# Attention with a mixture of experts: the order of work between the last query tile and the first routed tile

## What is computed

```python
attn = softmax(q_rounded @ k_rounded.T)          # per head, rows of 2048 keys
attn = round to 0..255 steps of the row's maximum
x = x + (attn @ v_rounded) @ Wp + bp
```

```python
logits = h @ router_w.T
scores = sqrt(softplus(logits)); idx = top_k(scores + expert_bias, 4)
out = sum over chosen e of share[e] * swiglu(h; gate_e, up_e, down_e)   # inner width 256
x = x + out + swiglu(h; shared weights)          # gate and up are clamped to +-7
```

## Time and profile before

| | us |
|---|---|
| median of 3 runs (1398.88 to 1402.76) | 1398.91 |
| profiled execution, reported time | 1404.4 |
| its span | 1402.7 |
| TensorE, VectorE busy | 1208.6 (86%), 1100.1 (78%) |
| ScalarE, GpSimd busy | 941.7 (67%), 884.2 (63%) |
| one gate copy (L902), one hidden product (L908), mean | 0.691, 0.453 |

### The profile page before, as it was taken

The page is one execution under the profiler, slowest core; times in us unless marked ns, Lnnn a source line. Parts: engine busy times, 40 slices in busy tenths (PEclk is TensorE's granted clock), DMA queues, the critical chain, the costliest instruction groups (busy, mean ns, idle before and its releaser), DMA issues.

```text
span 1402.7 us, 29359 instructions
## 1 busy us (share of the span) xinstructions
PE 1208.6 (86%) x7437; PEld 602.6 (43%) x7535; DVE 1100.1 (78%) x2282; ACT 941.7 (67%) x1349; POOL 884.2 (63%) x910
## 2 busy tenths in 40 slices
PE   7999577888888888888888855666999999999995
PEld 3444134444454444545444433333444444444442
DVE  4567899999999999999999964474667676767673
ACT  2224398999999999999999975212555555555552
POOL 3122388998889898989899972413445454545443
PEclk9999899999999999999999977877999999999997
DMA  7565878877777777767776773925678887787442
GB/s 256 127 152 128 165 128 159 151 144 154 141 140 147 153 148 145 147 145 142 146 153 135 158 176 101 305 29 205 134 204 214 248 231 172 183 243 187 86 66 30
DMA packets 401186, 220.10 MB, mean 157 GB/s; under 512 B 357335, under 2 KB 357463, under 8 KB 401122
## 3 DMA queue, kind: packets, MB, share of 16 engines
q1 hardware_dynamic: 380786, 180.51, 53.7%
q0 software_dynamic: 20336, 38.83, 15.5%
HBM read 101.88 MB, written 40.89 MB: 102 GB/s over the span
## 4 chain that ended last, share of the span: by engine, by line
PE 49%; issue 20%; DVE 14%; POOL 7%; ACT 5%; DMA 3%; SPq 1%; DVEq 0%; POOLq 0%; ACTq 0%
PE psS L1408 19%; PE psS L870 11%; DVE mem L623 5%; DVE mem L639 5%; POOL mem L713 4%; PE psS L474 4%; PE psS L1855 3%; ACT mem L580 3%; PE psAV L1842 1%; DMA mem<-mem 1%; PE psP L854 1%; PE psAV L520 1%; POOL mem L696 1%; PE psP L424 1%; PE psS L862 1%
## 5 line engine op out<-in xcount | busy, mean ns | idle before, releaser
L580 ACT ACTIVATE mem<-mem 128x2048 uint8<-128x2048 f32 x256 | 534.0, 2087 | 33.9 <-POOL mem L696 29.4
L713 POOL TENSOR_SCALAR mem<-mem 128x2048 bf16<-128x2048 uint8 x256 | 485.8, 1898 | 31.2 <-DMA mem<-mem 10.7
L474 PE MATMUL psS<-mem 128*128 128x512 bf16 x928 | 290.5, 387 | 88.0 <-DVE mem L639 36.8
L639 DVE TENSOR_SCALAR_CACHE_REDUCE mem<-psS,mem 128x1024 f32<-128x1024 f32 x256 | 327.3, 1279 | 3.5 <-PE psS L474 3.5
L623 DVE TENSOR_SCALAR_CACHE_REDUCE mem<-psS 128x1024 f32<-128x1024 f32 x256 | 312.3, 1220 | 12.8 <-PE psS L474 10.3
L1408 PE MATMUL psS<-mem 128*128 x624 | 296.1, 597 | 0.0
L1296 POOL DMA_INDIRECT out_y<-mem x78 | 123.5, 1584 | 191.9 <-DVE mem L1485 101.3
L870 PE MATMUL psS<-mem 128*128 (+1 forms) x376 | 191.2, 633 | 7.1 <-ACT mem L884 7.1
L494 PEld LDWEIGHTS psAV<-mem 128*128 128x128 bf16 x4096 | 139.4, 96 | 90.0 <-issue 26.6
L474 PEld LDWEIGHTS psS<-mem 128*128 128x128 bf16 x1024 | 72.2, 98 | 217.6 <-DVE mem L623 124.2
L902 DVE TENSOR_SCALAR mem<-psS 128x512 f32<-128x512 f32 x81 | 56.0, 691 | 138.2 <-PE psS L1408 117.1
(11 more groups left out here) (225 smaller groups left out, 1332.6 us busy)
## 6 DMA issues: line engine op xcount, KB each, us to landing
mem<-in_moe_w SPq DMA_DIRECT2D x64, 768.0 KB
xn_dram<-mem SPq DMA_DIRECT2D x29, 256.0 KB, 2.3
mem<-in_x SPq DMA_DIRECT2D x28, 256.0 KB, 3.0
mem<-xn_dram SPq DMA_DIRECT2D x19, 256.0 KB, 3.0
mem<-mem SPq DMA_TRANSPOSE x292, 3.1
mem<-in_ctx_in SPq DMA_DIRECT2D x16, 256.0 KB, 3.7
out_y<-mem SPq DMA_DIRECT2D x16, 256.0 KB, 2.2
gated_dram<-mem SPq DMA_DIRECT2D x13, 256.0 KB, 2.2
```

Source lines behind the costliest of these rows:

```text
L474: last = nc.tensor.matmul(psS[c][:, k * D:(k + 1) * D], qT[pm][:, hm, :], kT[:, hm, c * HALF + k * D:c * HALF + (k + 1) * D], start=True, ...
L580: nc.scalar.activation(p8[slot], S[slot], ACT.Exp, bias=NB[:, slot:slot + 1], scale=sq[p][:, h:h + 1], accum_out=Z[p][:, h:h + 1]).then_in ...
L639: nc.vector.tensor_scalar(S[before][:, HALF:TK], psS[1][:], 1.0, M[:, 2 * before:2 * before + 1], ALU.mult, ALU.max, accum_out=M[:, 2 * be ...
L713: nc.gpsimd.tensor_scalar(pb[slot], pT[slot].bitcast(U8).rearrange("p (j q b) -> p j b q", b=2, q=P), 1.0, 0.0, ALU.mult, ALU.add).then_in ...
```

## The change

On TensorE, the finish of tile 15 comes first in the run-out. The up product of tile 13 is made at l = 0, that of tile 14 at l = 14, that of tile 15 after the last step, all from the router's transposed rows xn2T and the weights gate_w that the attention stage uses; the reloads, `pe_tokens` and the copies for tiles 13 to 15 go. Of the other shared work only the transposes of hidden tile 0 (l = 7) and 1 (l = 28) stay in the run-out; the other hidden transposes and all sixteen down products come after it, with the ranks after k = 2, the ends after k = 5, and the lists 0 and 1 after k = 12 and k = 15. ScalarE takes the first tiles' softplus start ahead of unit 254's exponential. VectorE takes the clamps of tiles 0 to 3, the widening of unit 254, and the router of 13 tiles, then 3. GpSimd skips unit 254, clamps tile k + 6 ahead of add k. SP loads tiles 4 and 5 at l = 5, tiles 6 and 7 at l = 21, and tiles 8 to 12 with the first five experts after the up product of tile 15. Hidden products 6 to 9 take the places of 10 to 12 among the slot steps (7 one step later, 9 after the last sum). The ranks wait for x1 and gate 14, whose banks they use; all renumbered waits in the routed stage are left out here.

```diff
-    EARLY = 6
-    TA = TT - 2
+    TA = TT - 3
+    LAST = TT * H - 1
...
-                pe.wait_ge(probs_ready, n - LAG + 1)
+                if isinstance(n, int) and n - LAG == LAST - 1:
+                    pe.wait_ge(probs_wide, 1)
+                elif isinstance(n, int) and n - LAG == LAST:
+                    pe.wait_ge(probs_ready, LAST)
+                else:
+                    pe.wait_ge(probs_ready, n - LAG + 1)
...
+                if isinstance(t, int) and t >= TT:
+                    act.wait_ge(gu_mm, t - TT + 1)
                 nc.scalar.activation(xn2T.rearrange("p c t -> p (c t)"), psT[:], ACT.Copy).then_inc(router_ev, 1)
...
+            if isinstance(n, int) and n == LAST - 1:
+                act.wait_ge(logits_cp, TA)
+                nc.scalar.activation(absl[:, 0:TA, :], logits[:, 0:TA, :], ACT.Abs).then_inc(r_abs, 1)
+                act.wait_ge(r_abs, 1)
+                nc.scalar.activation(ex[:, 0:TA, :], absl[:, 0:TA, :], ACT.Exp, scale=-1.0).then_inc(r_exp, 1)
...
-            if not isinstance(n, int) or 0 <= n - BEHIND < TT * H:
+            if not isinstance(n, int) or 0 <= n - BEHIND < TT * H and n - BEHIND != LAST - 1:
...
+            if isinstance(k, int) and k < SHARED:
+                if due(k - 1):
+                    pe.wait_ge(hT_ready, k - 1)
+            else:
                 pe.wait_ge(hT_ready, k)
...
+        def bank_up(k):
+            return psT[:] if k == SHARED - 1 else psAV[0][:]
+
+        def pe_up(pe, k):
+            pe.wait_ge(router_ev, k + 1)
+            if k == GATED:
+                pe.wait_ge(x1_ready, TT - 1)
+            elif k == GATED + 1:
+                pe.wait_ge(gu_ready, 1)
             for c in range(DC):
-                last = nc.tensor.matmul(bankG[o], xT[o][:, c, :], w(c * 2 * I, 2 * I), start=(c == 0), stop=(c == DC - 1))
+                last = nc.tensor.matmul(bank_up(k), xn2T[:, c, :], gate_w[c], start=(c == 0), stop=(c == DC - 1))
             last.then_inc(gu_mm, 1)
...
+            if isinstance(k, int) and k < GATED:
+                return xg[k % MU]
+            return gu_third if isinstance(k, int) and k == SHARED - 1 else gu[o]
...
         def pe_early(pe):
             for l in range(PAIR):
                 pe_step(pe, TT // 2, l)
-                if l == 1:
-                    pe.wait_ge(shared_in, 16 * SHARED_PIECES)
+                if l == 0:
+                    pe_up(pe, GATED)
+                if l == LAG:
                     for c in range(2):
                         pe.wait_ge(half_max[c], TT * H)
-                if 2 <= l < 2 + 2 * EARLY:
-                    k = l // 2 - 1
-                    if l % 2 == 0:
-                        pe_hidden(pe, k, k % 2)
-                    else:
-                        pe_down(pe, k, k % 2, shared_weights)
-            pe.wait_ge(router_ev, TT)
-            pe.wait_ge(logits_cp, TT)
-            for k in range(EARLY, GATED):
+                    pe_hidden(pe, 0, 0)
+                if l == 14:
+                    pe_up(pe, GATED + 1)
+                if l == 28:
+                    pe_hidden(pe, 1, 1)
+            pe_up(pe, GATED + 2)
+            pe.wait_ge(shared_in, 16 * SHARED_PIECES)
+            pe_down(pe, 0, 0, shared_weights)
+            for k in range(2, SHARED):
                 pe_hidden(pe, k, k % 2)
-                if k > EARLY:
-                    pe_down(pe, k - 1, (k - 1) % 2, shared_weights)
-                if k == GATED - 4:
+                pe_down(pe, k - 1, (k - 1) % 2, shared_weights)
+                if k == 2:
+                    pe.wait_ge(logits_cp, TT)
+                    pe.wait_ge(x1_ready, TT)
+                    pe.wait_ge(gu_ready, 2)
                     pe_ranks(pe)
-            for k in range(GATED, SHARED):
-                o, before_o = k % 2, (k - 1) % 2
-                pe_tokens(pe, k, k % MU)
-                if k > GATED:
-                    pe_hidden(pe, k - 1, before_o)
-                pe_down(pe, k - 1, before_o, shared_weights)
-                if k == GATED:
-                    pe.wait_ge(hT_ready, GATED)
...
                 if l == 0:
-                    act.wait_ge(logits_cp, TA)
-                    nc.scalar.activation(first(absl), first(logits), ACT.Abs).then_inc(r_abs, 1)
-                    act.wait_ge(r_abs, 1)
-                    nc.scalar.activation(first(ex), first(absl), ACT.Exp, scale=-1.0).then_inc(r_exp, 1)
+                    act.wait_ge(r_plus, 1)
+                    nc.scalar.activation(first(lnu), first(u), ACT.Ln).then_inc(r_ln, 1)
+                if l == 1:
                     for k in range(2):
                         act_silu(act, k, k)
-                if 2 <= l < 2 + 2 * EARLY:
-                    k = l // 2 - 1
-                    if l % 2 == 0:
-                        act_hidden(act, k, k % 2)
-                        if k + 2 < EARLY + 1:
-                            act_silu(act, k + 2, k % 2)
-                    else:
-                        act_early_out(act, k)
-                if l == 3:
-                    act.wait_ge(r_plus, 1)
-                    nc.scalar.activation(first(lnu), first(u), ACT.Ln).then_inc(r_ln, 1)
-                if l == 7:
                     act.wait_ge(r_soft, 1)
                     nc.scalar.activation(first(score), first(full), ACT.Sqrt).then_inc(r_sqrt, 1)
+                if l == 4:
+                    act_hidden(act, 0, 0)
+                if l == 7:
+                    for k in range(2, 4):
+                        act_silu(act, k, k % 2)
+                if l == 27:
+                    act_hidden(act, 1, 1)
...
-            for k in range(EARLY, GATED):
+            act_early_out(act, 0)
+            for k in range(2, SHARED):
+                if k + 2 < SHARED:
+                    act_silu(act, k + 2, k % 2)
                 act_hidden(act, k, k % 2)
-                if k + 1 < GATED:
-                    act_silu(act, k + 1, (k + 1) % 2)
-                if k > EARLY:
-                    act_early_out(act, k - 1)
-            for k in range(GATED, SHARED):
-                act_tokens(act, k, k % 2)
-                if k > GATED:
-                    act_hidden(act, k - 1, (k - 1) % 2)
                 act_early_out(act, k - 1)
-                act_silu(act, k, k % 2)
-            act_hidden(act, SHARED - 1, (SHARED - 1) % 2)
             act_early_out(act, SHARED - 1)
...
+                dve.wait_ge(own_in[k], 16)
+                v_.tensor_scalar(xg[k][:, 0:D], xg[k][:, 0:D], 7.0, -7.0, ALU.min, ALU.max).then_inc(early_clamped, 1)
+
+            def widen(m):
+                slot = m % NS
+                dve.wait_ge(probs_moved[slot], 16 * (m // NS + 1))
+                dve.wait_ge(av_done, m - NS + 1)
+                v_.tensor_scalar(pb[slot], pT[slot].bitcast(U8).rearrange("p (j q b) -> p j b q", b=2, q=P),
+                                 1.0, 0.0, ALU.mult, ALU.add).then_inc(probs_wide, 1)
+
+            most, rest = slice(0, TA), slice(TA, TT)
             for l in range(PAIR):
                 dve_step(dve, TT // 2, l)
                 if l == 0:
-                    dve.wait_ge(logits_cp, TA)
                     dve.wait_ge(r_iota, 8)
+                    for k in range(MU):
+                        clamp(k)
+                    soft_first(most, 1)
+                    widen(LAST - 1)
+                    gate(GATED)
+                    soft_last(most, 1)
                     hidden(0)
                     hidden(1)
-                    soft_first(most, 1)
-                    hidden(2)
-                if l == 3:
-                    soft_last(most, 1)
-                    hidden(3)
-                if l == 7:
+                if l == LAG:
                     choose_first(most, range(0, TA), 1)
-                    hidden(4)
-                    choose_last(most, range(0, TA), {1: 5})
+                    choose_last(most, range(0, TA), {1: 2, 2: 3})
                     then(v_.tensor_scalar(token_id, count[:, 0:TT], float(P), part[:, 0:1], ALU.mult, ALU.add))
-            dve.wait_ge(av_done, TT * H)
-            dve.wait_ge(router_mm, TT)
-            dve.wait_ge(logits_cp, TT)
-            hidden(6)
-            soft_first(last_two, 2)
-            soft_last(last_two, 2)
-            choose_first(last_two, range(TA, TT), 2)
-            choose_last(last_two, range(TA, TT), {})
+                    gate(GATED + 1)
+            soft_first(rest, 2)
+            soft_last(rest, 2)
+            gate(GATED + 2)
+            choose_first(rest, range(TA, TT), 2)
+            choose_last(rest, range(TA, TT), {})
             dve.wait_ge(r_mask, 2)
-            hidden(7)
+            hidden(4)
             then(v_.tensor_tensor(prod, score, full, ALU.mult))
...
-                if j < SHARED - GATED:
-                    gate(GATED + j)
-                    name_of(j, 0)
-                    hidden(GATED + j)
-                else:
-                    name_of(j, 0)
+                name_of(j, 0)
```

(27 more changed lines are left out.)

76 lines of the change are left out of this document (35 added, 41 removed).

## The result

| | before | after |
|---|---|---|
| median of 4 runs (lowest to highest), us | 1398.89 (1396.79 to 1402.76) | 1360.26 (1357.77 to 1364.41) |
| profiled execution, us | 1404.4 | 1359.23 |
| its span, us | 1402.7 | 1357.5 |

The ratio is 0.9724, with a 95% interval of 0.9691 to 0.9757: 38.6 us faster, where 30.0 were forecast. (Ratios are of the means of the runs, times are medians.)

What follows compares the result with a forecast made beforehand. Bound by a chain of waits, no engine full, in the 143 us ahead of the routed stage. Gains 3.2 + 10.5 + 0 - 0.5 + 9.6 + 7.2 = 30.0; 1398.9 - 30.0 = 1368.9 us, range 1356 to 1387.

Steps and rivals of the forecast that it cites:

- Part 1: Last scores to scaled tile, 23.5 us before: steps move from GpSimd to VectorE; scaled at 840.0, gain 3.2 us.
- the rule of turns: Last scores to scaled tile: VectorE and GpSimd steps assumed to alternate; clamps done at 824.8, sums until 834.
- Part 2: Scaled tile to output product, 18.5 us before: shared products leave TensorE's path; gain 10.5 us, bounds 6.7 and 13.
- Part 3: Output product to logits, 7.9 us before: unchanged, tile 14's up product fits in TensorE's wait; gain 0.
- Part 4: Router choice, 8.3 us before: three tiles in place of two and a gate copy; 8.8 us, 0.5 lost.
- Part 5: Choice to slots, 24.1 us before: 14.5 us, paced by TensorE's shared tiles; gain 9.6 us, bounds 11 and 25.
- Part 6: Slots to list, 49.2 us before: reloads and up-product waits go, but load-paced shared tiles come late; 42 us, gain 7.2.
- Part 7: List to first up product, 10.7 us, and routed stage, 441 us: both unchanged.
- A: Rival: lower clock and the add loop eat most of the gain; list at 945, gain 6, time 1384; chance 0.22.
- B: Rival: VectorE is the floor, list-stage waits vanish and collisions are few; gain 42, time 1357; chance 0.09.
- C: Rival: slower, as all sixteen adds follow attention; at 6.0 us pace list at 967, time 1415; chance 0.06.
- D: Rival: gain hidden because the list waits for the experts' loads; time 1399; chance 0.05.

Runs made afterwards that it cites:

- three_ahead: Kernel after, with tile 0's down product made three extra times ahead of the last tile's transposes; 1366.59 us.
- quarter_up: Kernel before, without the row reloads of tiles 13 to 15 and with one of four chunks of their up products; 1388.88 us.
- after_again: Kernel after, unchanged, run again in a second series; 1363.17 us, ratio 0.9728.
- ranks_third: Kernel after, with the router's ranks one shared tile later; 1364.16 us.
- late_side: Kernel after, with ranks one tile later, second list product ahead of down product 13, gated rows and shares' store ahead of experts 1 to 4; 1359.96 us.
- loads_last: Kernel after, with the gated rows of tiles 8 to 12 loaded ahead of the first five experts; 1367.55 us.
- gathers_alone: Kernel after, with SP waiting for the first four gathers before it sends experts 5 to 7; 1358.32 us, ratio 0.9696.
- all_edits: both_sides with the wait of gathers_alone, and the first gathers ahead of GpSimd's last two adds; 1361.13 us, ratio 0.9708.
- widen_back: Kernel after, with unit 254 widened by GpSimd again; 1362.6 us.
- both_sides: late_side, with GpSimd clamping tiles 0 to 3 and VectorE scaling the last tile before gate 13, softplus end and hidden products 0 and 1; 1363.63 us.

## Why the prediction was right, and where it was wrong

The direction and the mechanism held, the time lies in the range, and the gain was 38.6 us instead of 30.0. Nearly all of the surplus lies in parts 1 and 6, and part 5 fell short. Parts 2 and 6 have an experiment behind them (three_ahead, quarter_up); what parts 1 and 5 gained is read from the two kernels' traces, and no run takes their edits apart. Gains in us, measured ones from the means of two profiles each:

| part | forecast | measured |
|---|---|---|
| 1. last scores to scaled tile | 3.2 | 6.8 |
| 2. to x1 | 10.5 | 10.0 |
| 3. to logits | 0 | 0.9 |
| 4. choice | -0.5 | -0.9 |
| 5. to slots | 9.6 | 8.3 |
| 6. to list | 7.2 | 12.6 |
| 7. to routed up product, and routed stage | 0 | -0.1, 1.1 |

**Part 1, mis-sized: the collisions.** I let the engines take turns, so that the clamps would end 5.1 us after the scores (824.8 less 819.7) and the sums 14.3 after. They ended 3.5 and 10.3 us after. From the sums' end to the scaled tile I had 6.0 us (its terms add up to 5.6) and 6.1 were measured, though split otherwise: the widening took 2.83, not 1.9. The error is the rule of turns itself. With 6.6 us of steps up to the sums' end it charged 7.7 us of collisions, and some 3.6 were paid. A short VectorE step that meets a widening of GpSimd ends just behind it, as the two rows I had said (828.68 and 831.30; I counted them as one); but behind it two short VectorE steps pass (818.87, 819.27) before the next widening starts, and the reciprocal passes beside a widening at no cost. So three collisions of some 1.6 us each were paid, the moved widening's among them. The scaled tile came 16.4 us after the scores, which is my bound for no collisions at all (836), so the bound was too high too. GpSimd's bias steps were late, as foreseen (0.57 and 0.52 instead of 0.27), and the last exponential came 6.1 us after the scores, 0.8 earlier than I had it. The Trainium skill ("SBUF — State Buffer", Who interferes with whom) describes a lock that the holder keeps for the length of a step. The trace agrees for these three steps, which ended 0.3 to 1.1 us after the widening they met.

**Part 2, right.** 8.0 and 9.2 us were measured, and the forecast is 8.5 by this mark (6.7 at the full clock, 1.3 for a slow start, and the 0.5 from the copy's start to the mark). The slow start is there: the first two residual products took 1.92 us, for the 1.02 that two such products take in three_ahead at the full clock (841.24). In after_again it lasts longer: the first four output products took 3.14 us, where the kernel after has 1.98, and that is most of the 1.2 us between the two. three_ahead shows from the other side that shared products in front of these steps cost two thirds or more of their length.

**Part 3, missed, small.** Before, TensorE stood 3.4 us before the normalized rows' transposes, and the router products behind them took 1.92 us (867.33); now the up product of tile 14 runs in that wait and they take 1.08. With the wait filled the clock was at its upper level. I had asked only whether the filler would stick out.

**Part 4, right** within 0.4: three tiles cost 0.9 more than two.

**Part 5, mechanism right, one wait not named.** The ranks followed at once, 0.4 us behind the choice. But as they stand ahead of the next shared tile, TensorE had nothing to do from 853.0 to 855.6, the ranks ran at the lower clock in 3.40 us for 1.80, and VectorE stood 2.81 us behind them at a hidden product. In after_again they took 1.80, VectorE stood 1.18 us, and the slots came after 15.1 and not 16.1 us; so about 1 us of the first profile's 1.6 us shortfall goes with the clock. ranks_third and late_side fill the gap with one more shared tile: 14.0 us, where I had forecast 14.5.

**Part 6, the step that failed.** Measured from SP's first gated load (forecast 865, came 855.8), the output copies of tiles 8 to 11 were forecast 24, 32, 36 and 37 us later and came 25.7, 31.3, 34.8 and 36.3 later: this part of the argument stood, and loads_last confirms that the loads set the pace. From the copy of tile 11 to the list I had 19 us (902 to 921); it was 14.6 (892.1 to 906.7). Two terms were too large. The three shared tiles from that copy to list 1 had 9 us (902 to 911) and took 6.9, until VectorE began the last names (898.96). The last list product and its reading had 3.5 us (917.5 to 921) and took 1.6. The names and places between were right (6.5 for 6.2). Nine us are 3 us a tile, between the 2.3 and 4.3 us that part 5 gives at the full and at half clock; the prediction doesn't say why. In this profile the products behind that copy took 1.88 to 1.95 us. That is 4.4 of the 6.6 us by which the first profile beats this part; another 1.6 is that the slots came 15.6 instead of 14 us after the first load, and the rest the copies. The second profile beats it by 4.4 us, of which 3.3 lie behind the copy of tile 11. quarter_up puts some 8 us of the stage's gain on the reloads and up products of the three tiles.

**Part 7, right,** but it was no constant of nature. Of the 10.7 us, 3.5 are the gathers waiting behind experts 5 to 7, as gathers_alone shows; I had looked only at what the gathers wait for, and not at what lies in the queues in front of them. The routed stage's 1.1 us I can't explain; it is no more than the kernels with the same code of that stage differ among themselves (439.7 to 441.1).

**The rivals.** A (the clock eats it) fell: the clock from slots to list was 0.95 in one profile and 0.86 in the other, and the list came 2.3 us later with the lower one. A's sum was also wrong: from 854 its parts add up to 939.5 and not 945, a gain of 11.5 and not 6. B was nearest in time (1357) and half right in mechanism: fewer collisions were paid than I had charged, but the waits on the loads did not vanish: VectorE still stands 6.4 us in the list stage, which loads_last shortens by another 3.7 to 6.0 us. C fell: the pace of the clamps was near its 6 us (5.7), but for five tiles only, and the last ten adds came 1.9 to 3.8 apart. D fell: the routed stage is no longer, even when experts come later still. Of the signs of being wrong, two showed once each in the first profile: a down product of 3.43 us (879.06) and two output copies 5.7 us apart (881.46, 887.13). The second was badly chosen, since the forecast itself has these two copies 8 us apart.

## What to carry to other kernels

When shared filler work moves, list for each queue what it now stands in front of: here the same microseconds moved from TensorE's order to SP's loads, then to the adds ahead of the gathers, and then into the routed stage, and each edit that looked at one queue alone was given back in the next, in part or in whole. Put the small transfer that the next stage waits for ahead of large loads that nobody needs yet; the one edit that by the marks gained without loss was such a wait, two lines long. Price a product behind a wait at both levels of the clock: here the same wait was followed by either, and it moved the slots by 1.0 to 1.9 us. And read a mark from two executions before you give its difference a cause.

## What was unexpected of the hardware

**A place step holds GpSimd's adds.** In the list stage an add's instruction takes 1.54 to 1.9 us. GpSimd's and VectorE's timelines of the kernel after show two that took twice that. GpSimd's:

```profile
896.14 3.46 POOL L1309 DMA_INDIRECT out_y<-mem,own_rows  x1 [0.30 <-issue]
...
903.60 2.99 POOL L1309 DMA_INDIRECT out_y<-mem,own_rows  x1 [0.30 <-issue]
```

VectorE's place steps:

```profile
895.90 2.28 DVE L1181 TENSOR_TENSOR mem<-count_h,mem 128x2048 f16<-128x2048 f16 x1
...
902.89 2.28 DVE L1181 TENSOR_TENSOR mem<-count_h,mem 128x2048 f16<-128x2048 f16 x1
```

Both adds ended 1.42 us after the place step that they met. In the fourteen profiles 28 adds begin during a place step: 25 ended 1.41 to 1.43 us after it, and three 2.06 or 2.07 us after. Those that begin up to 0.5 us ahead of one went either way: the add at 888.13 began 0.27 us ahead and had ended 0.8 us before the place step did, while two in all_edits began 0.5 us ahead and took 4.21 us, to 1.44 and 1.45 us after it. Name steps didn't hold an add: the one at 899.90 took 1.54, all of it within the names from 898.96 to 902.97. What I weighed in part 6 for the names thus happens in this kernel beside the long product of two inputs instead. It cost nothing in the kernel after, since the last add had ended (906.6) when the list was ready (906.7).

**The same short gap can cost the clock or not.** Six executions have the same products ahead of the ranks and the same wait of 2.4 us in front of them. In three (the kernel after, loads_last, gathers_alone) the 15 products took 3.40, 3.29 and 3.23 us, and in three (after_again, widen_back, three_ahead) 1.80. The slots came after 16.1 to 16.5 us in the first three and after 14.6 to 15.1 in the others. What decides it, these traces don't show. After gaps of 1.4 and 1.9 us (888.36, 884.78) the down products of the kernel after took 1.98.

**Landing depends on what was issued just before.** The first gathers landed after 3.7 us with no loads ahead of them and after 7.7 with six just issued; in both_sides, 4.1 us behind the loads, the first reached TensorE after 11.7, against 7.2 in the kernel after, where it was issued 1.5 us behind them.
